# Loads four groups ahead of attention, queries on a second queue, and shorter VectorE work around it

## The reference

```python
def _L0_xattn_ref(k, v, q, mask, Wk, bk, Wv, bv, Wq, bq, Wo, bo):      # 16 heads of 16
    kh = (k @ Wk.T + bk) ...; vh = (v @ Wv.T + bv) ...; qh = (q @ Wq.T + bq) ... / jnp.sqrt(HD)
    scores = jnp.where(mask, jnp.einsum('bhqd,bhkd->bhqk', qh, kh), -jnp.inf)
    return jnp.einsum('bhqk,bhkd->bqhd', softmax(scores), vh) @ Wo.T + bo
def _block(x, ...):                                                    # L0_ffn
    h = _layer_norm(x, ln1_g, ln1_b)
    q, k, v = jnp.split(h @ w_qkv, 3, axis=-1)
    x_resid = x + causal_attention(q, k, v) @ w_o                      # 16 heads of 16
    xf = _layer_norm(x_resid, ln2_g, ln2_b)
    probs = softmax(xf @ w_gate)                                       # 8 experts
    top_w, top_i = top_k(probs, 2); top_w = top_w / top_w.sum(-1)
    out = sum_e gate_e * (gelu(xf @ w1[e] + b1[e]) @ w2[e] + b2[e])    # hidden width 1024
    return out + x_resid
x = x + _L0_xattn_ref(ctx, ctx, _layernorm(x), ...)
x = x + _block(_layernorm(x), ...)
x = x + attention(_layernorm(x) @ Wq + bq, ctx @ Wk + bk, ctx @ Wv + bv)  # one head of 256, times 1/16
x = x + (silu(x @ gate) * (x @ up)) @ down                             # hidden width 768
```

## Time and profile before

| | us |
|---|---|
| median of 3 runs | 2400.95 (2400.32 to 2408.82) |
| profiled execution | 2402.38 |
| its span | 2400.4 |
| PE busy in the span | 1913.7 (80%) |
| DVE busy | 1491.0 (62%) |
| ACT busy | 1053.6 (44%) |
| POOL busy | 307.1 (13%) |

### The profile page before, as it was taken

How to read it: one execution, slowest core, us unless ns; L and a number is a source line. 1 busy time by engine, 2 the same in 40 slices (tenths; PEclk the granted TensorE clock), 3 DMA queues, 4 the chain that set the end, 5 groups by cost and what they waited for, 6 DMA issues and landing times. The chain is left out here.

```text
span 2400.4 us, 40323 instructions
## 1 busy us (share of the span) xinstructions
PE 1913.7 (80%) x13306; PEld 1144.1 (48%) x13307; DVE 1491.0 (62%) x3004; ACT 1053.6 (44%) x1974; POOL 307.1 (13%) x348
## 2 busy tenths in 40 slices
PE   7846999997488269999846618999999647998997
PEld 4501222222355135555335417888888524554555
DVE  5845888884488347777458656544444356666753
ACT  3404777776133036666501116433333235554552
POOL 1000000000433000000022142111111131221000
PEclk9958999999699579999966659999999868999999
DMA  6742444420577534444166325211111321111100
GB/s 204 268 141 83 111 107 108 106 76 30 147 253 245 164 94 132 132 132 114 35 167 164 94 92 198 95 51 46 44 53 44 100 70 36 56 58 46 35 10 18
DMA packets 211807, 249.44 MB, mean 104 GB/s; under 512 B 41920, under 2 KB 163544, under 8 KB 211664
## 3 DMA queue, kind: packets, MB, share of 16 engines
q1 hardware_dynamic: 182848, 199.35, 27.5%
q10 hardware_dynamic: 22000, 29.66, 4.4%
q0 software_dynamic: 6816, 18.62, 2.8%
HBM read 155.18 MB, written 90.78 MB: 102 GB/s over the span
## 5 line engine op out<-in xcount | busy, mean ns | idle before, releaser
L803 ACT ACTIVATE a_prob<-a_psE 128x512 f32<-128x512 f32 (+3 forms) x1024 | 480.9, 521 | 375.7 <-PE a_psE L723 187.3
L699 PE MATMUL a_psS<-a_K,a_Q 97*128 97x512 bf16 (+3 forms) x1024 | 359.7, 357 | 97.1 <-DMA a_V<-s_v 32.6
L723 PE MATMUL a_psE<-a_Q,a_K 100*128 100x512 bf16 (+3 forms) x1024 | 350.1, 346 | 48.4 <-DMA a_Q<-a_nrow 26.8
L836 DVE TENSOR_REDUCE a_nm<-a_psS 128x2 f32<-128x1024 f32 x256 | 308.2, 1216 | 101.0 <-PE a_psS L699 100.4
L833 DVE TENSOR_REDUCE a_nm<-a_psS 128x1 f32<-128x128 f32 (+3 forms) x512 | 227.2, 481 | 119.0 <-PE a_psS L702 118.6
L1553 PE MATMUL ex_psY<-ex_w2h,ex_hl 128*128 x1872 | 230.4, 273 | 12.5 <-DVEq L1448 12.4
L1539 PE MATMUL ex_psH<-ex_xT,ex_w1h 128*128 128x256 f16 x1872 | 233.8, 275 | 3.4 <-ACT ex_xT L1487 2.1
L736 PE MATMUL a_psO<-a_prob,a_V 128*32 128x512 f32 (+3 forms) x2048 | 232.9, 527 | 2.0 <-ACT a_prob L803 1.4
L1497 ACT ACTIVATE ex_hf<-ex_psH,ex_b 128x256 f32<-128x256 f32 x312 | 130.7, 470 | 222.0 <-PE ex_psH L1539 217.8
L723 PEld LDWEIGHTS a_psE<-a_Q,a_K 100*128 100x128 bf16 x1024 | 100.1, 98 | 255.8 <-ACT a_prob L803 143.4
L699 PEld LDWEIGHTS a_psS<-a_K,a_Q 97*128 97x128 bf16 x1024 | 100.9, 100 | 244.8 <-DVE a_nm L833 42.2
(11 more groups left out here) (269 smaller groups left out, 2799.6 us busy)
## 6 DMA issues: line engine op xcount, KB each, us to landing
s_qk<-t_parts SPq DMA_DIRECT2D x64, 384.0 KB, 3.4
s_v<-t_vaug SPq DMA_DIRECT2D x16, 1024.0 KB, 6.4
a_V<-s_v SPq DMA_DIRECT2D x64, 256.0 KB
s_o<-a_oT SPq DMA_DIRECT2D x64, 256.0 KB, 2.2
ex_stage<-in_w SPq DMA_DIRECT2D x16, 1024.0 KB
a_K<-s_qk SPq DMA_DIRECT2D x64, 192.0 KB
a_Q<-s_qk SPq DMA_DIRECT2D x64, 192.0 KB
s_ys<-ex_yo SPq DMA_DIRECT2D x39, 256.0 KB, 2.6
```

The lines of the kernel that those rows point to most:

```text
L699: last = pe.matmul(bank[:, 0:n], Q6[s][0:K_MAX, h, t * P:(t + 1) * P], K6[s][0:K_MAX, h, 0:n], start=True, stop=not causal)
L723: last = pe.matmul(bank[:, 0:S - q0], K6[s][0:K_EXP, h, t * P:(t + 1) * P], Q6[s][0:K_EXP, h, q0:S], start=True, stop=not causal)
L803: act.activation(prob[j % NP_BUF][:, 0:n], psE[ring(G, j) % NE][:, 0:n], ACT.Exp).then_inc(p_ready, 1)
L836: dve.tensor_reduce(nm[s % NM_BUF][:, t - 1:t + 1, h], psS_all[:, (j - 1) % NS:j % NS + 1, :], axis=AX.X, op=ALU.max, negate=True).then_in ...
```

## The change

In attention, the loads are four groups ahead (`AHEAD`) rather than seven. SP issues loads 0 to 2, the shift rows of group 0 in one transfer, load 3, and in step G the result of G-1, the shift rows of G+1, the load of G+4 and the reciprocals of G-1. The queries of groups 0 to 3 are issued on ScalarE's queue. V is laid out in memory so that its load is 128 rows of 2 KB, and has its own semaphore, on which TensorE waits only before the first product with V.

In the token stages loops are written out, inputs have three buffers (`NIN`), and x, x1, y1 and base lie in memory in rows of 4 KB per partition rather than 1 KB. In t1 the division goes to VectorE, between the two splits, and the bias becomes one more matmul per tile of tokens. In t2 the division goes to VectorE too; gates, ranks, the b2 product and their stores are removed; normalisation with gain and offset becomes two scalar_tensor_tensor per tile; the logits stay on the chip. The expert stage takes the two largest logits of all tokens at once on VectorE, takes one exponential for the gates, and adds b2, loaded once per tile, where a tile's result leaves TensorE. In the last stage the loop is written out.

```diff
-            def divide(n, par):
-                for k in range(DC):
-                    pool.wait_ge(c_in[par], (n - par) * (2 * DC * 8) + 2 * DC * 16)
-                    pool.tensor_tensor(cin[par][:, k, :], cin[par][:, k, :], rb[par][:, k, :], ALU.mult
-                                       ).then_inc(div_done, 1)
-            def add_bias(n, par):
-                pool.wait_ge(x_in[par], (n - par) * 8 + 16)
-                pool.tensor_tensor(xin[par][:], xin[par][:], bo[:].unsqueeze(1).to_broadcast([P, TT, D]), ALU.add
-                                   ).then_inc(bias_done, 1)
...
-            def body(n, par):
+            for n in range(1, B):
                 deviations(n)
-                divide(n + 1, 1 - par)
-                add_bias(n + 1, 1 - par)
...
+            def divide(n):
+                k = n % NIN
+                dve.wait_ge(c_in[k], (n // NIN + 1) * (2 * DC * 16))
+                dve.tensor_tensor(cin[k][:].rearrange("p c s -> p (c s)"), cin[k][:].rearrange("p c s -> p (c s)"),
+                                  rb[k][:].rearrange("p c s -> p (c s)"), ALU.mult).then_inc(div_done, 1)
...
+            if stage == 1:
+                dve.memset(bo_rows[:], 0.0)
+                dve.memset(bo_ones[:], 1.0)
+                link(dve.tensor_copy(bo_part[0][:], bo[:]))
+                link(dve.tensor_tensor(bo_rest[:], bo[:], bo_part[0][:], ALU.subtract))
+                link(dve.tensor_copy(bo_part[1][:], bo_rest[:]))
+                dve.tensor_copy(bo_rows[0:1, :], bo_part[0][0:1, :])
+                dve.tensor_copy(bo_rows[32:33, :], bo_part[1][32:33, :])
+                dve.tensor_tensor(bo_rows[64:65, :], bo_rest[64:65, :], bo_part[1][64:65, :], ALU.subtract
+                                  ).then_inc(bias_set, 1)
+                divide(0)
+            front(0, 0, lambda: divide(1))
             link.reset()
...
+                        pe.matmul(psV[t][:, 0:D], cin[n % NIN][:, g, t * P:(t + 1) * P], wo[:, g, :],
+                                  start=g == 0, stop=False)
+                    pe.matmul(psV[t][:, 0:D], bo_ones[:], bo_rows[:], start=False, stop=True).then_inc(v_ps, 1)
                 pe.drain().then_inc(c_used, 1)
...
+    AHEAD = 4
...
+    v_in = [c.sem(f"v_in{s}") for s in range(SLOTS)]
...
+    def key_rows(G, s, r):
+        m, g = NPART - r, G % NG
+        src = scr["qk"][ds(G // NG * DC + g // 2, 1), 0, 0:m].rearrange("o t (d e h) n -> (o t d) e (h n)", d=HD, e=2)
+        return K6[s][FIRST_ROW[r]:FIRST_ROW[r] + m * HD].rearrange("p h n -> p (h n)"), src[:, g % 2, :]
+    def query_rows(G, s, r):
+        m, g = NPART - r, G % NG
+        src = scr["qk"][ds(G // NG * DC + g // 2, 1), 1, r].rearrange("o (d e h) n -> (o d) e (h n)", d=HD, e=2)
+        return (Q6[s][FIRST_ROW[r]:FIRST_ROW[r] + m * HD].rearrange("p h n -> p (h n)"),
+                src[:, g % 2, :].unsqueeze(0).to_broadcast([m, HD, GH * S]))
...
         def _(sp):
             def load(G, s):
-                if not (isinstance(G, int) and G < SLOTS):
+                if G >= SLOTS:
                     sp.wait_ge(oT_ready, G - SLOTS + 1)
...
                 for r in range(NPART):
-                    m = NPART - r
-                    src = scr["qk"][ds(row, 1), 0, 0:m].rearrange("o t (d e h) n -> (o t d) e (h n)", d=HD, e=2)
-                    sp.dma_start(K6[s][at:at + m * HD].rearrange("p h n -> p (h n)"), src[:, half, :]
-                                 ).then_inc(g_in[s], 16)
-                    src = scr["qk"][ds(row, 1), 1, r].rearrange("o (d e h) n -> (o d) e (h n)", d=HD, e=2)
-                    sp.dma_start(Q6[s][at:at + m * HD].rearrange("p h n -> p (h n)"),
-                                 src[:, half, :].unsqueeze(0).to_broadcast([m, HD, GH * S])
-                                 ).then_inc(g_in[s], 16)
...
-                sp.dma_start(V[s][:], scr["v"][ds(b, 1), :, g * GH * HP:(g + 1) * GH * HP]
-                             .rearrange("o (t p) c -> p (o t) c", p=P)).then_inc(g_in[s], 16)
+                    sp.dma_start(*key_rows(G, s, r)).then_inc(g_in[s], 16)
+                    if G >= AHEAD:
+                        sp.dma_start(*query_rows(G, s, r)).then_inc(g_in[s], 16)
                 if not causal:
                     sp.dma_start(K6[s][KM:KM + 1, :, :],
-                                 scr["mask"][ds(b, 1), :].unsqueeze(1).to_broadcast([1, GH, S])
+                                 scr["mask"][ds(G // NG, 1), :].unsqueeze(1).to_broadcast([1, GH, S])
                                  ).then_inc(g_in[s], 16)
-            for G in range(SLOTS // 2):
-                load(G, G)
-            def maxima(G, s):
+                sp.dma_start(V[s][:].rearrange("p t c -> p (t c)"), scr["v"][G // NG, G % NG]).then_inc(v_in[s], 16)
+            def shift_in(G, s):
                 sp.wait_ge(nrow_ready, G + 1)
-                for r in range(NPART):
-                    sp.dma_start(Q6[s][KM + 1 + r:KM + 2 + r, :, :],
-                                 nrow[s % 2][r * GH:(r + 1) * GH, :]).then_inc(nrow_in[s % 2], 16)
+                sp.dma_start(Q6[s][KM + 1:KM + 1 + NPART].rearrange("r h n -> r (h n)"), nrow[s % 2][:]
+                             ).then_inc(nrow_in[s % 2], 16)
...
-            maxima(0, 0)
-            for G in range(SLOTS // 2, SLOTS):
+            for G in range(AHEAD - 1):
                 load(G, G)
+            shift_in(0, 0)
+            load(AHEAD - 1, AHEAD - 1)
             def step(G, s):
+                if G > 0:
+                    result(G - 1, (s - 1) % SLOTS)
                 if not last_of(G, 1):
-                    maxima(G + 1, (s + 1) % SLOTS)
-                if isinstance(G, int) and G == 0:
-                    return
-                result(G - 1, (s - 1) % SLOTS)
-                if not last_of(G, SLOTS - 1):
-                    load(G + SLOTS - 1, (s - 1) % SLOTS)
-                inverse(G - 1, (s - 1) % SLOTS)
+                    shift_in(G + 1, (s + 1) % SLOTS)
+                if not last_of(G, AHEAD):
+                    load(G + AHEAD, (s + AHEAD) % SLOTS)
+                if G > 0:
+                    inverse(G - 1, (s - 1) % SLOTS)
...
                 if t == 0:
                     pe.wait_ge(oT_ready, G)
+                    pe.wait_ge(v_in[s], (G // SLOTS + 1) * 16)
...
+                pe.wait_ge(nrow_in[s % 2], (G - s % 2) * 8 + 16)
...
+                act.dma_start(*query_rows(0, 0, r)).then_inc(g_in[0], 16)
             act.wait_ge(rows_set, 1)
             k0 = 0 if causal else 1
             for s in range(SLOTS):
+                if 0 < s < AHEAD:
+                    for r in range(NPART):
+                        act.dma_start(*query_rows(s, s, r)).then_inc(g_in[s], 16)
...
-            def divide(n, par):
-                for k in range(DC):
-                    pool.wait_ge(c_in[par], (n - par) * (2 * DC * 8) + 2 * DC * 16)
-                    pool.tensor_tensor(cin[par][:, k, :], cin[par][:, k, :], rb[par][:, k, :], ALU.mult
-                                       ).then_inc(div_done, 1)
...
+            def divide(n):
+                k = n % NIN
+                dve.wait_ge(c_in[k], (n // NIN + 1) * (2 * DC * 16))
+                dve.tensor_tensor(cin[k][:].rearrange("p c s -> p (c s)"), cin[k][:].rearrange("p c s -> p (c s)"),
+                                  rb[k][:].rearrange("p c s -> p (c s)"), ALU.mult).then_inc(div_done, 1)
...
+                dve.wait_ge(var_ready, n + 1)
+                for t in range(TT):
+                    last = dve.scalar_tensor_tensor(out=half[:, t, :], in0=xres[:, t, :], scalar=mv[:, t, 0:1],
+                                                    in1=lng[:], op0=ALU.subtract, op1=ALU.mult)
+                link(last)
...
-                link(dve.tensor_tensor(base[par][:], xres[:], xin[par][:], ALU.add))
+                for t in range(TT):
+                    last = dve.scalar_tensor_tensor(out=y[par][:, t, :], in0=half[:, t, :], scalar=rstd[:, t:t + 1],
+                                                    in1=lnb[:], op0=ALU.mult, op1=ALU.add)
+                last.then_inc(y_ready, 1)
+                dve.wait_ge(base_out[par], (n - par) * 8)
+                dve.tensor_tensor(base[par][:], xres[:], xin[k][:], ALU.add).then_inc(base_ready, 1)
+                dve.wait_ge(base_ready, n + 1)
                 dve.sem_inc(x_used, 1)
...
-            def experts(n, par):
...
+                act.wait_ge(tr_ps, n + 1)
+                act.wait_ge(yT_used, n)
+                act.copy(yT[:].rearrange("p c s -> p (c s)"), psT[:]).then_inc(yT_ready, 1)
+                if n + NIN < B:
+                    load(n + NIN)
+                act.wait_ge(l_ps, n + 1)
+                act.copy(logits[:, ds(n * TT, TT), :].rearrange("p t e -> p (t e)"), psL[:, 0:TT * E_N]
+                         ).then_inc(l_free, 1)
...
+            def choose(scores, best, chosen):
+                link(dve.tensor_reduce(best[:], scores[:], axis=AX.X, op=ALU.max))
```

(29 more changed lines are left out.)

497 lines of the change are left out of this document (191 added, 306 removed).

## The result

The changed kernel takes 2259.25 us (median of 4 runs, 2255.46 to 2260.28) against 2403.64 for the kernel before, measured beside it (4 runs). The ratio is 0.9395, with an interval of 0.9372 to 0.9417: 6.0% faster. The prediction was 2253, with a range of 2218 to 2295. The profiled execution has a span of 2253.7 us against 2400.4, 146.7 less; the sum of the prediction was 147.5. The total is right, but some of its terms are not, and they cancel: t1 brought 8.5 us too little, and t2 and la 8.7 us too much.

A forecast was written before the change was run, and what follows sets the result against it. TensorE bounds the attention (apart from holes), expert and last stages, VectorE the token stages. Terms -0.5-27.5-17-32-66+1-5.5 = -147.5 us take 2402.4 to 2254.9, 2253 on the median's scale; range 2218 to 2295.

The forecast's parts named there:

- t1: Token stage between the attentions: division and bias leave GpSimd, shortening VectorE's batch; -17 us, between -10 and -20.
- t2: Token stage after the second attention: removed VectorE work shortens batches and the end; -66 us, between -50 and -76.
- la: Last stage: writing out the loop removes VectorE's idle at the back-edge; -5.5 us, between 0 and -6.
- The attention holes: TensorE's idle at both attention starts: fewer loads ahead of the shift rows shorten it, -27.5 and -32 us.
- a0: First attention stage: step 0 at +34 and step 1 at +47 us; -27.5 us, between -21 and -36.
- a1: Second attention stage: step 0 at +33.5 and step 1 at +43.5 us; -32 us, between -23 and -40.
- The 8.4 us a group: Attention loads: time per group between steps 0 and 1, expected to stay because the query loads keep their broadcast shape.
- the tail: End of t2, from last residual to stage end: 43.3 us before, 16 after; -27 us.
- the load's term: In t2, writes half hidden make a batch 12.2 us, not VectorE's 10.8; 7 x (17.8 - 12.2) = -39 us.
- ex: Expert stage: no wait for gates, but more VectorE operations to choose experts; +1 us, between -2 and +3.
- The smaller gain: Rival: step 0 stays, t2 load-bound at 14.6 us a batch, t1 at -10; -109 us, 2293 us; chance 0.18.
- Four ahead too few: Rival: attention loads stretch past 15 us, each of 62 steps pays; 2441 us at 3 us each; chance 0.03.

The follow-up runs named there:

- the old order alone: The changed kernel with SP's earlier issue order in attention (loads 0 to 3, shift rows of group 0, loads 4 to 7, then seven ahead): 2305.15 us.
- the copies apart: The changed kernel with each query copy its own transfer, not one led by a broadcast: 2244.22 us; with SP's earlier issue order too, 2268.53 us.
- the division early: The changed kernel with query copies as their own transfers and t1's division on VectorE ahead of both splits: 2234.06 us, ratio 0.9293 to the kernel before.
- the one with an earlier first batch: The changed kernel with t2's second batch divided after the first batch's normalisation, not ahead of its residual: 2259.11 us, t2 118.0 us.

## Why the prediction was right, and where it was not

**The attention holes (a0 -27.5, a1 -32).** Right in the mechanism. The argument was the place of the shift rows behind the loads; the old order alone brings back holes of 18.70 and 21.55 us, and the order carries 52 of 59 us. The 8.4 us a group was right too, and was the more important number: it also says how far ahead the loads must be. That the two stages came out within 0.4 us is partly luck. Step 1 starts 2 us later than forecast in both. This came back from a term that the working did not have: before, step 1 began at the lower clock after its hole, and took 2.4 us more than it does now in a0 and 1.7 in a1. And the forecast of step 0 took a whole group, 8.4 us, for the order, which moves step 0 by 3.2 and 3.0 us. In a1 the other 5.6 of 8.6 us come from the rest of the change, which was priced at nothing.

**The queries' queue and V's semaphore (nothing).** Right that they gain nothing: +0.4 and -2.4 us without the queue, +0.3 and +1.0 without the semaphore. The Trainium skill, page "DMA: Bandwidth & Descriptors", section "Issuing engines are not separate DMA queues", says as much of the first, and the experiment agrees that nothing is gained; the 2.4 us that the queue costs in a1 were not foreseen. If the parts add up, the 2.7 and 4.5 us that the order leaves belong to V's long rows or the single transfer of the shift rows, which were priced at nothing as well. No run takes either back alone, so this stays open. In the kernel before, the load of V released the first scores of a1; in the changed kernel it does not.

**What makes a group 8.4 us.** The prediction left it as a rate. The experiments with the copies apart show that it is the shape: the same bytes in transfers that have 16 rows in front rather than a broadcast of 3 or 2 take 5.1 us a group in a1 and 5.6 in a0, where SP's issuing alone takes 4.6 and 5.3. The Trainium skill, page "DMA: Bandwidth & Descriptors", section "Why a DMA increments its semaphore by 16 and not by 1", gives the slowest dimension larger than 1 as what sets the number of engines; the fall from 8.4 to 5.1 agrees with it. The prediction counted the load with a single copy among the slow ones, but that one has 16 rows in front in both kernels. The runs do not count the engines themselves.

**t1 (-17, measured -8.5).** The step that failed is the one that took VectorE's saving for the batch's. It holds on VectorE, where the product with rstd is 1.14 us in all batches. But the working left TensorE out as having "65 us of idle", and at 17.4 us a batch little of that is left: TensorE's own chain is 17.9 - 1.5 = 16.4 us. The division stands between the splits, TensorE waits 1.54 us for it, and a batch takes 17.9. Six batches make 3 us. The start is 1.5 us later (the first statistics at +26.6 against +25.1). The wait for the constants, to +15.8, was there before too, but the set-up of the bias rows then takes 2.2 us and stands ahead of the division; I took 0 for the start. And 3.3 us are the lower clock, in the last batch's projection and its values' product (5.41 for 3.69), where TensorE had become the bound and pays for it. This part differs between executions: with nothing changed in t1 the stage takes 189.5 to 194.4 us, and one to three of its batches take 19.5 us. The three make 7.8 of the 8.5 us that are missing. With the division early a batch takes 17.1 us, which shows the first of the three; the start and the clock are read from the timelines alone. "The change takes these off GpSimd: -4.1" was also one price for two things: on GpSimd the division alone costs VectorE 1.9 us by overlap and saves it 1.2, so moving it was worth 0.7 us of VectorE's time a batch and nothing of the stage's, which is 6 us shorter with the division on GpSimd. The bias addition was the better half of the gain.

**t2 (-66, measured -72.3).** Right in the removed work, and in the tail (15.8 us from the last residual to the end, forecast 16). Mis-sized was the load's term: "if the writes hide half I get 12.2 us". They hide nearly whole: most batches are 10.6 us, and VectorE's own sum in the prediction was 10.8. From the first to the last statistics the stage takes 73.7 us, before 125.0: -51.3 where I had -39. Against it stands +6.6 at the start, which the prediction did not name: the second batch's division is ahead of the first residual. Moving it gains nothing, as the loads are then waited for. So the loads stand just behind VectorE: the bound of 10.8 in the prediction was where the stage lies, and in other executions, most of all in the one with an earlier first batch, single batches wait for their loads again.

**ex (+1, measured +2.3) and la (-5.5, measured -7.9).** The operation that marks the chosen experts starts 2.7 us later in its stage than before. Both stages vary by 4 to 5 us from one execution to the next, so neither difference is told from its forecast.

**The rivals.** The smaller gain would have had a0 and a1 at -21 and -23; step 0 moved, by 4.6 and 8.6 us, so it fell. Four ahead too few: no step waits for a load at four, each pays 6.9 us at three. The margin was real but near: the failure was one group away and costs 420 us, far beyond the 147 gained.

## What to carry to other kernels

A small transfer on which the next step depends should be issued ahead of bulk loads that are not needed yet; to find how few loads may stand before it, divide the hole by the groups that were loaded in it, and compare that rate with the step. Before moving loads to another queue, look at the DMA share while an engine waits for them: here, at 0.30, changing the shape of the transfers gained 14.7 us in attention and the queue nothing. A wait of TensorE can cost more than its length: look at the granted clock of the work behind it. When an engine's share of a stage is cut, write down the next engine's own chain, waits for the moved work included, since that is what the saving is measured against.
